# Zero products behind each collect, and the transposed maxima in another PSUM bank: the attention layers of a graph network

## The reference

```python
h = (x @ W).reshape(n, HEADS, HID)                 # 4 heads of 64
a_s = einsum('nhc,hc->nh', h, att_src)
a_d = einsum('nhc,hc->nh', h, att_dst)
e = leaky_relu(a_s[src] + a_d[dst], 0.2)
m = segment_max(e, dst)
ex = exp(e - m[dst])
alpha = ex / segment_sum(ex, dst)[dst]
out = segment_sum(h[src] * alpha[:, :, None], dst) + b
```

## Time and profile before

| what | us |
|---|---|
| median of 3 runs (4389.03 to 4397.5) | 4394.04 |
| span of the profiled execution | 4836.3 |
| first attention layer, steady part of it | 1278.0 |
| second attention layer, steady part of it | 1270.0 |
| TensorE busy, over the whole span | 3107.3 |
| VectorE busy | 3044.1 |
| ScalarE busy | 2574.7 |
| GpSimd busy | 2895.1 |

### The profile page before, as it was taken

One profiled execution on the slowest core, in us unless ns is written; L12 is line 12 of the kernel. 1 busy time (PEld: TensorE's weight loads), 2 busy tenths in 40 slices (PEclk: granted clock), 3 DMA queues, 4 the chain that ended last, 5 costly groups with the idle time before them and its releaser, 6 DMA issues. The chain is left out here.

```text
span 4836.3 us, 56702 instructions
## 1 busy us (share of the span) xinstructions
PE 3107.3 (64%) x11125; PEld 1876.3 (39%) x11125; DVE 3044.1 (63%) x8069; ACT 2574.7 (53%) x7729; POOL 2895.1 (60%) x2918
## 2 busy tenths in 40 slices
PE   4699999989998883455555555555354555555451
PEld 3344444444444372333333334433233333333331
DVE  7788888878887753455555455566354555555557
ACT  3598888888888642333334334344243334343347
POOL 2366666656665405677777767733676777777763
PEclk8899999999999996677777767778576777767776
DMA  5233323333322244444444444424444444444445
GB/s 165 93 88 87 86 86 86 87 85 86 87 85 84 72 127 134 112 129 118 129 123 124 129 118 129 131 61 127 117 126 121 122 125 128 118 129 124 124 108 161
DMA packets 274567, 540.54 MB, mean 112 GB/s; under 512 B 73156, under 2 KB 161983, under 8 KB 274240
## 3 DMA queue, kind: packets, MB, share of 16 engines
q0 software_dynamic: 134912, 376.36, 28.8%
q1 hardware_dynamic: 132308, 154.29, 10.3%
q10 hardware_dynamic: 7020, 6.40, 0.4%
HBM read 495.47 MB, written 41.31 MB: 111 GB/s over the span
## 5 line engine op out<-in xcount | busy, mean ns | idle before, releaser
L1247 POOL DMA_INDIRECT arena<-h_rows,idx x1856 | 1893.8, 1020 | 972.0 <-issue 515.2
L1382 PE MATMUL ps<-arena,z 128*128 128x264 f32 x3712 | 1328.7, 511 | 493.1 <-DVE arena L1494 290.8
L769 POOL DMA_INDIRECT arena<-y_rows,idx x928 | 901.0, 971 | 717.7 <-ACT arena L800 359.1
L1306 ACT ACTIVATE z<-z 128x256 f32<-128x256 f32 x928 | 382.2, 412 | 1504.0 <-remote 833.3
L1382 PEld LDWEIGHTS ps<-arena,z 128*128 128x128 f32 x3712 | 856.6, 249 | 728.2 <-DVE arena L1494 351.7
L1502 DVE TENSOR_TENSOR z<-ps,z 128x264 f32 x928 | 396.1, 427 | 1105.3 <-remote 713.3
L798 ACT ACTIVATE arena<-arena 128x128 f32<-128x128 f32 x2784 | 912.0, 393 | 110.8 <-DVE arena L885 64.4
L840 PE MATMUL ps<-arena 128*128 128x512 f32 x1856 | 902.5, 610 | 4.6 <-DVE z L893 4.6
L1298 ACT ACTIVATE z<-iota,dst_x 128x128 f32<-128x128 f32 x1856 | 644.5, 395 | 26.4
L1494 DVE TENSOR_TENSOR arena<-arena,z 128x520 f32<-128x520 f32 x928 | 639.0, 689 | 1.8 <-ACT z L1287 1.1
L832 PE MATMUL ps<-arena 128*128 128x512 f32 x928 | 495.6, 617 | 121.2 <-DVE arena L885 85.2
(11 more groups left out here) (231 smaller groups left out, 2838.3 us busy)
## 6 DMA issues: line engine op xcount, KB each, us to landing
z<-lo_rows SPq DMA_DIRECT2D x116, 512.0 KB
arena<-h_rows,idx POOLq DMA_INDIRECT x1856
arena<-y_rows,idx POOLq DMA_INDIRECT x928
z<-seg_rows SPq DMA_DIRECT2D x232, 64.0 KB
h_rows<-arena SPq DMA_DIRECT2D x98, 132.0 KB, 1.8
arena<-h_rows SPq DMA_DIRECT2D x98, 132.0 KB, 3.0
arena<-res_rows SPq DMA_DIRECT2D x98, 128.0 KB, 3.0
z<-in_ea_rows SPq DMA_DIRECT2D x464, 8.0 KB
```

What stands on the lines that cost most here:

```text
L769: pool.indirect_dma_start(out=ring[:, r, :], out_offset=None, in_=s.y_rows, in_offset=bass.IndirectOffsetOnAxis(ap=rows_of[:, u, n:n + 1], ...
L1247: pool.indirect_dma_start(out=ring[:, u * SCORED + n, :], out_offset=None, in_=h_rows, in_offset=bass.IndirectOffsetOnAxis(ap=s.idx[:, u, ...
L1306: nc.scalar.activation(sel[:, q % SELS, :, :].rearrange("p k n -> p (k n)"), away[:, q % 2, :, :].rearrange("p k n -> p (k n)"), ACT.Relu, ...
L1382: last = t.matmul(ps[:, bank[q % 4], 0:ROW], sel[:, q % SELS, k, :], ring[:, u * SCORED + 2 * q + k, :], start=(k == 0), stop=(k == 1))
```

## The change

At the end of each of the 16 steps of a group TensorE gets two more products: 128 columns of zeros as weights, 512 columns of zeros as the moving side, in bf16, with bank 5 as their target, which nothing reads. They have no wait and signal nobody. The zeros lie in the first half of `s.w8`, which VectorE clears at the start of each layer. The transposed maxima and the line move from bank 5 to bank 3, behind the scores and the scale factors.

```diff
-    scT, scale_ps, max_ps, row_ps = ps[:, 3, 0:P], ps[:, 3, P:P + HEADS], ps[:, 5, 0:P], ps[0:1, 5, P:2 * P]
+    scT, scale_ps, max_ps, row_ps = ps[:, 3, 0:P], ps[:, 3, P:P + HEADS], ps[:, 3, 2 * P:3 * P], ps[0:1, 3, 3 * P:4 * P]
+    spare, fill = ps[:, 5, :], s.w8[:, 0:4 * HID].bitcast(BF16)
...
                         if 0 <= q - 1 < STEPS_IN // 2:
                             look_up(g + 1, 1 - u, 2 * (q - 1))
                             look_up(g + 1, 1 - u, 2 * (q - 1) + 1)
+                    for _ in range(2):
+                        t.matmul(spare, fill[:, 0:P], fill, start=True, stop=True)
...
+            v.memset(s.w8[:, 0:4 * HID], 0.0)
             step(v.tensor_copy(parts[:, :, 0, :], s.asd[:, :, :]))
```

## The result

The changed kernel takes 4424.36 us (median of 4 runs, 4422.87 to 4426.20); the kernel before took 4391.99 us beside it. The ratio is 1.0074, with a 95% interval of 1.006 to 1.0088: slower by 32 us. I had forecast 4400 us, with a range of 4310 to 4500 us and 0.35 for slower by over 0.2%. My own case, gathers hide the fills, had a range of 4386 to 4418 us, and the measured time lies outside that one.

What follows compares the result with a forecast made beforehand. GpSimd's gathers were taken to bound the steady groups and hide the fills there; sharing and memset cost nothing, the two layers' tails +6 us, so 4394 + 6 = 4400 us, range 4310 to 4500 us.

Steps and rivals of the forecast that it cites:

- My own case: Whole kernel: waits for gathers hide the fills except in the tails; 4400 us, range 4386 to 4418, chance 0.60.
- What bounds: Attention layers' steady groups: GpSimd's gathers alone take 42.8 us of 46; compute needs 25.6 us when nothing holds it.
- The sharing and the memset: Maxima moved to bank 3: cost 0. Clearing zeros at each layer's start: 0.21 us, hidden under the first gathers.
- The fill's price: One 512-column bf16 product on TensorE: 0.21 us at the high clock, 0.43 us a pair.
- The tail: After each layer's last gather: TensorE with fills sets the pace at 1.37 us a pair, +3.0 us a layer.
- The steady groups: The 56 groups ahead of each layer's last: compute with fills, at most 39.3 us, fits under 42.8 us of gathers; 0 us.
- the ring rival: Gathers wait for a slot freed by collect, in the median run too: +150 us, 4544 us, +40 about as likely; chance 0.20.
- The signs: Steady groups 46 us, gathers 0.30 us apart, TensorE busy up 7 to 14 us; final pairs 1.3 to 1.4 us apart.
- Slower by more than 0.2%: Whole kernel slower by over 8.8 us, through a longer tail or the ring rival: chance 0.35.
- The rival of a clock that pays: Attention layers: clock stays up and compute sets the pace; -156 us, 4238 us, half of it (4316 us) likelier; chance 0.20.
- One reading of the clock: In the profile before, TensorE's clock was read as 0.50 again from 3020.4, after 4.2 us of standing.

Runs made afterwards that it cites:

- disturbed trace: First profile of the unchanged kernel, on which the prediction rests: span 4836.3 us, against its 4394.04 us median.
- second profile: The kernel before, profiled again with no edit: 4393.40 us, ratio 1.0001, span of the profiled run 4383.7 us.
- the batch: Changed kernel with one fill a pair, with 128-column fills, or with a group's 32 fills in one row, none in the last group: 4392.41, 4391.60, 4391.24 us.

## Why the prediction was right and where it was off

**What bounds.** Right: GpSimd's gathers set the pace of the steady groups, and 0.95 us with 0.30 us between is what a free gather costs. My 42.8 us a group came from a disturbed trace; undisturbed it is 41.7 us. The 7.6 us a group by which I put the median below the profile was too much: I shared the whole 442 us out among the groups, but in the second profile the first gather of the attention layers starts 187 us earlier (1663.3 for 1850.6), so that much lies in the convolution, and the groups differ by 4.5 us (46.2 to 41.7).

**The sharing and the memset.** Right, 0: the sharing alone measures 1.0000. The memset ran only together with fills, in versions at 0.9996 to 1.0000.

**The fill's price.** Right: 0.22 us at the high clock, for my 0.21.

**The tail.** Right in mechanism and size for the change as a whole. I had written that TensorE takes over the pace at 1.37 us a pair, for +3.0 us a layer; it came to +2.7 and +2.9. In the changed kernel's last group collects start 1.32 us apart:

```profile
2909.36 1.05 PE L1383 MATMUL ps<-arena,z 128*128 128x264 f32 x4
2910.25 0.59 PE L1399 MATMUL ps<-w 128*128 128x512 bf16 x2
2910.68 1.05 PE L1383 MATMUL ps<-arena,z 128*128 128x264 f32 x4
```

My sum took the clock of 1.00 there as given. With fills in the last group alone the clock is 0.50 at first, and the tails are 5.7 and 4.4 us longer.

**The steady groups.** This is the step that failed: "So 0 us in the 56 groups ahead of the last of each layer, which gathers pace." I asked only whether the compute side, with fills, still fits under the gathers. It does, and TensorE stands for some 14 us a group for want of gathered rows, with and without fills. In the changed kernel:

```profile
L1362 PE MATMUL ps<-ident,z 128*128 128x128 f32 x58 | 27.5, 475 | 825.1 <-ACT z L1280 825.1
L1280 ACT ACTIVATE z<-arena 128x128 f32<-128x128 f32 x58 | 24.9, 430 | 892.3 <-DMA arena<-h_rows,idx 892.3
```

What I left out is that the gathers' own time depends on VectorE. I had the evidence: gathers of 1.02 us on average beside single ones of 0.95. That 0.07 us a gather was 2.2 us of every 46 and I didn't ask where it came from. The term of the sum was 0 and measures +0.55 us a group, 32 us in all (0.48 us, 27 us, against the trace with the bank shared alone).

**The number.** That 4424 us lies in the stated range is luck. My own case ended at 4418 us, and what reached past it was the room that I had given to the ring rival, which didn't happen.

**The signs.** Gathers with 0.30 us between them, the last group's pairs 1.32 us apart and the fill at 0.22 us came as written. TensorE's busy time went up by some 4 us a group (21.28 to 24.89 us in the group shown), not by 7 to 14: collects took less time at the higher clock, and some records of the fills are missing (1706 of 1856). A group of 46 us was a figure of the disturbed trace.

**Slower by more than 0.2%** had 0.35, but by a longer tail or by the ring; neither was the cause. The ring rival is out: no gather waits for its slot, the longest gap between two in a layer being 0.32 us. The rival of a clock that pays is out as well: the clock rose as forecast (0.82 in the steady part, for 0.75 to 0.85), and the batch got it higher for nothing. One reading of the clock was off: it fell at 3020.4, inside the stand of 4.19 us that ended at 3021.35, not behind it.

**Open.** Why two fills meet more messages than none, one or three is told here by rows, not by a rule that would have said so ahead; my one attempt at such a rule missed. Nor was it tried what would free the one-hot compare, which holds 0.5 us of the group that is left.

## What to carry to other kernels

When the queue that sets the pace is GpSimd's, read the spread of its instructions and not only their sum: here the mean above the shortest was contention, and a change on TensorE that only re-timed VectorE moved it. Keeping TensorE's clock up was worth nothing where TensorE waited for data; it showed in the tails alone, where nothing was gathered any more. Where a VectorE product with two SBUF operands runs beside GpSimd's gathers, move one operand to PSUM: that was worth 1.4% here, at no cost in VectorE's time.

## What the hardware did that I had not expected

A gather that begins while a two-operand SBUF product of VectorE runs ends 0.82 us after that product, for any remainder over 0.13 us, unless the one-hot compare comes right behind; one that begins 0.09 us ahead of the product is not held at all. So whether a message holds a gather is decided at the gather's start.

The one-hot compare is otherwise. In the rows of 1766.07 it begins 0.70 us into a gather, 0.27 us after the message's end, and the gather still ends 0.3 us late, 0.12 us after the compare; so in all 54 steady groups. And the hold goes both ways: in the second profile of before the 50 compares that begin 0.52 to 0.59 us into a gather take 0.87 to 0.94 us, and the 66 others 0.74 us in the median.

The cost isn't monotone in the number of fills: 1.0000, 1.0074 and 0.9994 for one, two and three a pair.

The first profile of before lay 10% above the timed runs, with look-ups 1.7 us apart and all engines starting again together. In the second profile of the same kernel there is none of this, and no gather waits. The prediction took those stretches for a cost of being profiled; but the second execution was profiled too, so profiling alone doesn't bring them. A span that doesn't match the timed runs was the sign to trust its durations of single instructions and not its waits. What caused them stays open.
